# Layer 0 of a graph network: the products that pick node rows spread as 8, 7, 8, 7 chunks over four steps, in two parts per step

## What is computed

```python
def _L0_gnn_ref(x, edge_index, edge_attr, W1, b1, W2, b2):
    src, dst = (edge_index[0], edge_index[1])
    x_i = x[dst]
    x_j = x[src]
    tmp = jnp.concatenate([x_i, x_j, edge_attr], axis=1)
    h = jax.nn.relu(tmp @ W1 + b1)
    msg = h @ W2 + b2
    out = jax.ops.segment_sum(msg, dst, num_segments=N_NODES)
    return out

def _L1_gnn_ref(node_feat, edge_feat, src, dst, eps):
    m = jax.nn.relu(node_feat[src] + edge_feat)
    neigh = jax.ops.segment_sum(m, dst, num_segments=N_NODES)
    return (1.0 + eps[0]) * node_feat + neigh
x = _layernorm(x + _L0_gnn_ref(x, edge_index, edge_attr_32, ...), axis=-1)
x = _layernorm(x + _L1_gnn_ref(x, edge_attr_48, src, dst, L1_gnn_eps), axis=-1)
```

## Time and profile before

| | us |
|---|---|
| median of 3 runs | 4232.41 |
| lowest and highest run | 4227.96, 4232.42 |
| span of the profiled execution, first to last instruction | 4179.9 |
| median less span | 52.5 |
| layer 0, its steady part with products | 258 to 1795 |
| layer 1 | 2240 to 4179 |

### The profile page before, as it was taken

The page is one execution under the profiler, slowest core; times in us unless marked ns, Lnnn a source line. Parts: engine busy times, 40 slices in busy tenths (PEclk is TensorE's granted clock), DMA queues, the critical chain, the costliest instruction groups (busy, mean ns, idle before and its releaser), DMA issues.

```text
span 4179.9 us, 58888 instructions
## 1 busy us (share of the span) xinstructions
PE 3719.5 (89%) x21330; PEld 2937.4 (70%) x21330; DVE 2153.2 (52%) x4308; ACT 661.6 (16%) x1275; POOL 2550.7 (61%) x2692
## 2 busy tenths in 40 slices
PE   5798998889998998999998898988888898889998
PEld 3576676667776776777776777777777777767777
DVE  2343433433443433434445666666666666666665
ACT  1222222212222222222221000000000000001111
POOL 5666666666666666656653666666666666666664
PEclk7698989989899998889997999999999999999988
DMA  5222222222222222222221222222222222222221
GB/s 104 33 36 34 34 34 36 34 34 36 34 34 36 34 36 33 35 33 37 41 36 35 48 49 49 46 49 48 48 49 48 49 49 46 49 49 47 52 54 43
DMA packets 408203, 178.79 MB, mean 43 GB/s; under 512 B 279084, under 2 KB 407074, under 8 KB 407810
## 3 DMA queue, kind: packets, MB, share of 16 engines
q0 software_dynamic: 86016, 66.23, 11.6%
q1 hardware_dynamic: 319778, 108.26, 11.2%
q10 hardware_dynamic: 2114, 0.49, 0.1%
HBM read 169.74 MB, written 5.00 MB: 42 GB/s over the span
## 4 chain that ended last, share of the span: by engine, by line
PE 41%; another core or an unknown queue 23%; DVE 19%; issue 13%; POOL 2%; DVEq 1%; DMA 1%; ACT 0%; SPq 0%; POOLq 0%
PE ps_t L869 9%; PE ps_h L869 8%; PE ps_early L869 7%; DVE picked L1087 6%; PE ps_out L776 5%; PE ps_as L768 4%; PE ps_h L827 4%; DVE at_place L1078 4%; DVE edge L997 3%; PE ps_t L794 2%; POOL edge L554 2%; PE ps_nodes L879 2%; DVE acc L1011 2%; DVE pre L1111 1%
## 5 line engine op out<-in xcount | busy, mean ns | idle before, releaser
L554 POOL DMA_INDIRECT edge<-x,resid_sb x1430 | 1357.5, 949 | 863.4 <-issue 402.8
L554 POOL DMA_INDIRECT edge<-x_dram,resid_sb x1258 | 1193.0, 948 | 743.0 <-issue 378.9
L869 PE MATMUL ps_t<-x_parts,at_place 125*128 125x480 f32 x3040 | 768.1, 404 | 47.1 <-issue 45.7
L869 PE MATMUL ps_h<-x_parts,at_place 125*128 125x480 f32 x3080 | 757.5, 400 | 33.2 <-issue 27.1
L869 PE MATMUL ps_early<-x_parts,at_place 125*128 125x480 f32 x2680 | 733.9, 422 | 48.3 <-DVE edge L997 31.2
L1078 DVE TENSOR_TENSOR at_place<-place_row,ps_out 125x1280 fp32r<-125x1280 f32 x440 | 651.7, 1481 | 168.4 <-remote 150.8
L869 PEld LDWEIGHTS ps_t<-x_parts,at_place 125*128 125x128 f32 x3040 | 593.5, 199 | 177.7 <-issue 81.9
L869 PEld LDWEIGHTS ps_h<-x_parts,at_place 125*128 125x128 f32 x3080 | 605.3, 199 | 147.7 <-issue 42.6
L869 PEld LDWEIGHTS ps_early<-x_parts,at_place 125*128 125x128 f32 x2680 | 519.9, 196 | 251.7 <-issue 136.2
L1033 DVE COPY w_edge<-ps_as 48x128 f32<-48x128 f32 x391 | 112.5, 288 | 831.0 <-remote 752.0
L768 PE MATMUL ps_as<-edge,msg 128*48 128x48 f32 x6256 | 355.2, 219 | 165.6 <-ACT msg L696 74.5
(11 more groups left out here) (64 smaller groups left out, 1662.1 us busy)
## 6 DMA issues: line engine op xcount, KB each, us to landing
e_sb<-e SPq DMA_DIRECT2D x196, 192.0 KB
place_row<-rows_dram SPq DMA_DIRECT2D x440, 62.5 KB
edge<-e SPq DMA_DIRECT2D x196, 128.0 KB
edge<-x,resid_sb POOLq DMA_INDIRECT x1430
edge<-x_dram,resid_sb POOLq DMA_INDIRECT x1258
x_win<-xT SPq DMA_DIRECT2D x391, 9.0 KB
acc<-xT SPq DMA_DIRECT2D x10, 234.4 KB
feats<-x SPq DMA_DIRECT2D x10, 234.4 KB
```

The costliest lines, as they stand in the source:

```text
L554: pool.indirect_dma_start(out=cols, out_offset=None, in_=rows_of, in_offset=bass.IndirectOffsetOnAxis(ap=index, axis=0)).then_inc(done, 16)
L869: last = nc.tensor.matmul(banks[q % len(banks)], lhsT=at_place[:, q % PLACED, c, :], rhs=x1_parts[:, c, part, :], start=(c == 0 and part = ...
```

## The change

plan_pairs now lays the products in pieces with a place: place 1 stands in front of the segment sums, place 2 at the end of the step, where all were before. The first pick has chunks 3 and 5 in A and 2 in B (place 1). The second has 5 in B (place 2) and 5 in C (place 1). The third has 3 in C (place 2), 3 in D (place 1) and 4 in D (place 2). The steps so have 8, 7, 8 and 7 chunks. The groups that get picks move: pairs s+3, s+4 and s+5 have one, where it was s+2, s+3 and s+5. The steps in which places are found stay the same. VectorE selects the first pick in B and the second in C, both behind the comparisons of 997, and the third in the next A, at the front as before. GpSimd waits for the end of the front part at a pair's second gather; its waits for the output and hidden layers move back by one gather; the rear part gives two signals.

```diff
-        for begin, end in ((s, s), (s + 1, s + 1), (s + 2, s + 3)):
+        for pieces in (((s, 1, 3), (s, 2, 5), (s + 1, 1, 2)), ((s + 1, 2, 5), (s + 2, 1, 5)), ((s + 2, 2, 3), (s + 3, 1, 3), (s + 3, 2, 4))):
+            begin, (end, part, _) = pieces[0][0], pieces[-1]
             if end >= last:
                 continue
-            q, each = len(picks), CHUNKS // (end - begin + 1)
-            for step in range(begin, end + 1):
-                units[step] = [(q, (step - begin) * each + c) for c in range(each)]
-            picks.append((2 * (end + 2) + 1, begin - 1, end + 1))
+            q, c = len(picks), 0
+            for step, place, n in pieces:
+                units[step, place] = [(q, k) for k in range(c, c + n)]
+                c += n
+            picks.append((2 * (end + 2) + 1, begin - 1, (end, 1) if part == 1 else (end + 1, 0)))
...
-THIRDS0 = {u[k] for u in PRODUCTS0.values() for k in thirds_of(u)}
+ENDS0 = {u[k] for (_, place), u in PRODUCTS0.items() for k in ((len(u) - 1,) if place == 1 else (len(u) // 2, len(u) - 1))}
...
                 if k == 0:
                     wait_for(pool, S0["awin"], p)
-                elif k == 1:
+                elif k == 1 and (p, 1) in PRODUCTS0:
+                    pool.wait_ge(S0["third"], parts_before(p, 1) + 1)
+                elif k == 2:
                     wait_for(pool, S0["msgp"], 2 * p - 4)
-                elif k < 4:
-                    wait_for(pool, S0["pre"], 2 * p - 4 + k)
-                elif k < 7 and p >= 0 and thirds_of(PRODUCTS0.get(p, ())):
-                    pool.wait_ge(S0["third"], thirds_before(PRODUCTS0, p) + k - 3)
+                elif k in (3, 4):
+                    wait_for(pool, S0["pre"], 2 * p - 5 + k)
+                elif k in (5, 6) and (p, 2) in PRODUCTS0:
+                    pool.wait_ge(S0["third"], parts_before(p, 2) + k - 4)
...
+                if p == FIRST_PICK:
+                    pe.wait_ge(S0["parts"], PARTS * PIECES)
+                pick_rows(S0, PRODUCTS0.get((p, 1), ()), [ps_early])
                 for g in pair(p - 3):
                     sum_messages(S0, g)
...
-                products = PRODUCTS0.get(p, ())
+                products = PRODUCTS0.get((p, 2), ())
...
             def steps0(p):
-                for q, (_, _, select) in enumerate(PLAN0):
-                    if select == p:
-                        select_rows(S0, PLAN0, q, [ps_early])
+                select_at((p, 0))
...
                 for g in pair(p + 1):
                     onehots(S0, g, iota_sb[:, :])
+                select_at((p, 1))
```

More of the change, by code:

```diff
@@ L561, in thirds_before, with parts_before @@
                 return sum(len(thirds_of(u)) for s, u in products.items() if 0 <= s < step)
+            def parts_before(step, place):
+                return sum(place_of for s, place_of in PRODUCTS0 if s < step or s == step and place_of < place)
             def in_step(g, k):
@@ L805, in steps0 @@
                         edges_there(p)
-                    if not PRODUCTS0.get(p - 1):
+                    if not PRODUCTS0.get((p - 1, 2)):
                         wait_for(pe, S0["onehot"], pair(p)[-1])
@@ L828, in steps0 @@
                                      start=True, stop=True).then_inc(S0["pre"], 1)
-                if p == FIRST_PICK:
-                    pe.wait_ge(S0["parts"], PARTS * PIECES)
-                products = PRODUCTS0.get(p, ())
+                products = PRODUCTS0.get((p, 2), ())
                 pick_rows(S0, products[:-1], [ps_early])
@@ L865, in pick_rows @@
                     for part in range(PARTS):
-                        if part:
-                            if (q, c) in (THIRDS0 if S is S0 else THIRDS):
-                                last.then_inc(S["third"], 1)
+                        if part and (q, c) in (ENDS0 if S is S0 else THIRDS):
+                            last.then_inc(S["third"], 1)
                         last = nc.tensor.matmul(banks[q % len(banks)], lhsT=at_place[:, q % PLACED, c, :], rhs=x1_parts[:, c, part, :],
@@ L1038, in zero_sums, with select_at @@
                 nc.vector.tensor_copy(by_chunk(acc)[:, bass.ds(c, 1), :], zeros[:, :].unsqueeze(1).to_broadcast([D, 1, CN])).then_inc(S0["zeroed"], 1)
+            def select_at(place):
+                for q, (_, _, select) in enumerate(PLAN0):
+                    if select == place:
+                        select_rows(S0, PLAN0, q, [ps_early])
             def steps0(p):
-                for q, (_, _, select) in enumerate(PLAN0):
-                    if select == p:
-                        select_rows(S0, PLAN0, q, [ps_early])
+                select_at((p, 0))
                 if p == 3:
```

## The result

The kernel before has a median of 4232.41 us in 4 runs (4227.96 to 4235.38), the changed kernel 4343.44 us in 4 runs (4324.19 to 4349.82). The ratio is 1.0261, with a 95% interval of 1.0235 to 1.0287: **2.6% slower**, 111 us. The forecast was 4308 us, within 4100 to 4480.

A forecast was written before the change was run, and what follows sets the result against it. TensorE, busy for 89% of the span, was taken as the bound. A round of four steps (A to D) was 36.3 + 5.7 stalls + 4.3 clock = 46.3 against 44.6 us; over 44.75 rounds +76, so 4308 us, range 4100 to 4480.

The forecast's parts named there:

- The wait on the bank: A new sum's first product in B and C waits for VectorE's selection from the one PSUM bank: +5.7 us a round.
- the formula for its length: Stall = d + 2.8 - 3.1 us; d runs from the segment sums' end to VectorE's first copy.
- two stalls of 2.8 us: TensorE idle ahead of the rear products, once in B and once in C; together +5.7 us, bounds 1.4 and 13.8.
- d of 3.4: Middle of three lags from segment sums' end to first copy (1.0, 3.4, 7.2 us), giving stalls of 0.7, 2.8, 6.9.
- the front products of A: Their wait for VectorE's places replaces the segment sums' wait for messages, of the same length; no added cost.
- The floor: A round of four steps when nothing waits: 35.9 us plus 0.4 for extra starts, 36.3 us.
- The 35.9 from single steps: Round without waits at clock 1.00: 10.1 + 10.1 + 7.85 + 7.85 us, from single steps with 20 and 10 products.
- the block starts: Each step now has two product blocks; an extra start taken at 0.1 us, +0.4 us a round.
- The clock: TensorE's clock falls to its lower level once a round, as before the change: 4.3 us; granted clock at or below 0.90.
- 44.75 equal rounds: Products of layer 0 in steps 14 to 192, each round costed at +1.7 us, together +76 us.
- the signal is prompt: Rival: d about 1 us in B and C, stalls 1.3 us together; 4112 us, without clock falls 3919; chance 0.32.
- 52.5 us between span and median: The runs' median lies 52.5 us above the profiled span of 4179.9 us; left as is, with 4232.4 as base.

The follow-up runs named there:

- late setting: Group of follow-up runs (chip 7) in which the kernel before has a median of 4212 us, close to the first measurement's 4232 us.
- prompt setting: Two groups of follow-up runs (chips 13 and 9): kernel before at a median of 3493 us, the change at 3565.41 us, ratio 1.0210.
- late copy kernel: Changed kernel with VectorE's first copy in steps 16 to 149 held until the step's last hidden-layer matmul; 4451.16 us, 1.0559 of the kernel before.

## Why the prediction was right, and where its steps were off

**The wait on the bank** was named rightly, and the formula for its length holds in four steps of two kernels. But the two stalls of 2.8 us were in truth 5.8 and 0.3: that their sum comes out right (6.1 for 5.7) is luck. I put the same d of 3.4 into B and C. Measured over the steady part, d is 6.0 us on average in B and 0.3 in C. Behind the long stall in B, TensorE's signals are prompt in C; that the stall lets them catch up fits the rows, but no run shows it by itself. For B the late end of my bounds, 6.9 us, was nearer than the middle one. And a third place was missed. I let the front products of A wait for their places, as the segment sums had waited for the messages, and saw only the sums of B and C on the bank. But the third pick's sum ends at the end of D and the next begins in A's front part, with only transposes and a window matmul between: 1.5 us a round.

**The floor** of 36.3 us was 0.5 too low: where nothing waits and the clock stays at 1.00 the round takes 1269.5 / 34.5 = 36.8 us. The 35.9 from single steps was near (1244.9 / 34.5 = 36.1 busy in the kernel before), and the block starts, put at 0.4, cost 0.7.

**The clock** was put at 4.3 us a round. Measured: TensorE is busy 1391.2 / 34.5 = 40.3 us a round against 36.8 at full clock, 3.5 us. The granted clock of the steady part rose from 0.90 to 0.92, where I had expected 0.90 or less. The level falls 40 times in the 34.5 rounds, 31 of them in B, and of 5.6 us at the lower level in a B 1.5 lie in the stall itself, where they cost nothing. In the kernel before it fell 34 times, 17 in A and 13 in D.

**The sum.** 36.8 + 3.5 of clock + 7.3 of idle time ((1642.7 - 1391.2) / 34.5) = 47.6 us, against 46.3 forecast. Of the 7.3 us, 5.1 stand ahead of the rear products of B, 1.4 ahead of the front products of A, 0.2 in C, and 0.5 are waits for the comparisons. The step that was mis-sized most is the stall of B, and with it C's and A's. That the time came within 1% of the forecast is in part luck, since these misses go both ways.

**What went away** as forecast: the transposes' wait for gathers, 0.0 us.

**The steps from 158 on** had no term of their own. I took 44.75 equal rounds. In the late setting that was harmless, +27 us in 8.75 rounds, 3.1 a round as elsewhere. In the prompt setting it is nearly all of the loss, 49 of 73 us, and it is the clock (0.88 against 0.99). The profile of before couldn't show this cost: one small matmul more a step was enough to lose 50 us there.

**The rival "the signal is prompt"** is what the prompt setting shows in the steady part, but measured against a kernel before that has prompt signals as well: 36.8 us a round against 36.3. I had reckoned it as a gain of 2.7 to 7.0 us a round against 44.6. That step was wrong. Where the signals are prompt, the old waits and the falls of the clock are gone from the kernel before too (busy 1244.9 of 1252.9 us at 1.00); there was nothing left to gain, and the change is slower in both settings. My other doubt, that the modelled ends of matmuls might be too early, is answered there as well: from 300 to 1400 us of the changed kernel nearly all signals come 0.013 to 0.015 us after the modelled end. The chance of 0.32 for a gain rested on pricing one side only.

**The time around the span.** I laid 52.5 us between span and median. The changed kernel's profiled run has a span of 4339.4 and a time of 4341.24 us: only 1.8 lie outside. The profiled execution of before was most likely a quicker one than those timed. The median was the better base, but for another reason than I gave.

## What to carry to other kernels

When a sum is moved so that it ends and the next begins inside one step, follow the release of its bank through the reader's whole queue: what stands ahead of the reader, and which signal of the waiting engine itself that waits for. Price the first stall of such a loop by the longest lag seen in the trace, and the one right behind it by a short one: here they were 6.0 and 0.3 us. If a rival says that a lag is really small, take it out of the kernel before as well before writing down a gain. And measure the time of the profiled execution against the timed runs before using its span as a base.

## What the runs showed of the hardware that I had not expected

**Signals of TensorE that arrive together and late.** In the late setting the semaphore events of TensorE are held back and come in a burst. Each of the three parts sends two signals. In one B of the late copy kernel, times in us from the start of the window matmul, with the modelled ends of the matmuls that signal:

```
segment sums end     2.03  2.25      signals  7.10  7.19
output layer ends    3.27  4.16      signals  7.28  7.38
hidden layer ends    5.09  5.95      signals  7.42  7.46
```

In the same step of the changed kernel in the prompt setting:

```
segment sums end     2.05  2.27      signals  2.07  2.29
output layer ends    3.30  4.19      signals  3.31  4.20
hidden layer ends    5.12  5.97      signals  5.13  5.99
```

There are 3.70 us from the last signal of the sums to the last of the hidden layer where signals are prompt. In the steps B of the changed kernel as first measured it is 0.27 us in the median (29 of 34 steps, in which all four are recorded), too short for the output and hidden layers to be done in between. So at least the first of these signals were held back, and it isn't the work that was late. It shows in the rows as well: the copy and ScalarE's relu start within 0.23 us (1407.57 and 1407.80). In A and D it is 0.27 us in the median too; in C, behind the long stall, it is 3.70. What holds the signals back stays open. The granted clock alone isn't it, for in the A from 1387.30 us, at 1.00, the copy starts 3.8 us after the sums.

**The setting is worth more than the change.** The same kernel before takes 3493 us on two chips and 4212 us on a third, 21% more, and the change costs 2.1% in the one and 2.6% in the other, mostly from different places: the steps from 158 on there, the stalls of the steady part here. That the late signals make all of the 21% is not shown.

**A clock that falls without a wait.** One more small matmul a step, 8 us of work in all, made the kernel before 54.5 us slower (3547.16 against 3492.65). In the 35 steps from 158 on, in which TensorE never waited, the granted clock fell 10 times instead of once.
